# New orders of work for the steps of an attention pipeline that runs over five engines of one core

## Chip, core and metric

One NeuronCore of a Trainium2 chip runs the whole program in one launch. The metric is the device time of one execution in microseconds, median of several. The kernel before takes 427.58 us (three runs, 427.24 to 427.79). A time on the profile's clock is counted from the start of the profiled execution's span.

## What is computed

A pre-norm decoder layer over `x` of 64 sequences by 64 positions by 128 channels, in float32:

```python
x = x + attention(layernorm(x), Wv, bv, Wo, bo)        # q = k = v = layernorm(x) @ Wv.T + bv, 16 heads of 8
x = x + cross_attention(layernorm(x), ctx, ctx)        # 16 heads of 8, no projections
x = x + experts(layernorm(x), router, ...)             # one shared expert and the best one of seven, SwiGLU, 352 wide
```

Each attention is a softmax over 64 keys per head, with the scores divided by the root of the head's width.

## The kernel before

Two sequences make a **unit** of 128 rows (`U` = 32 units). The program has a first stage, both attentions and the normalised rows of the third part for all units (the profile's first 233 us, with a drain to about 262 us), and a second stage, routing and experts (to 427 us). The change is in the first stage alone.

The first stage is a software pipeline written out by hand: `phase_a` calls `body(t, u, live)` on each engine for steps t = 0 to 32, and in step t each part of the work is done for the unit t minus its lag:

```python
LAG = {"norm": 0, "xT": 0, "proj": 1, "S_s": 1, "soft_s": 2, "out": 3, "xb": 3, "q": 4, "pv_x": 5, "on_x": 6, "st_x": 7}
```

Every engine takes its instructions strictly in the order in which its own `body` issues them, and engines wait for one another by semaphores. That order, one list per engine, is all that decides how the work interleaves. `sp`, `pool`, `pe`, `act` and `dve` below are the DMA queue's engine, GpSimd, TensorE, ScalarE and VectorE.

The parts of a step, with the lines of the profile and the tiles:

- **Self attention.** TensorE turns the normalised row (`xT`, L778), projects it (L802 and L809, into `ps_v` and `ps_pT`), ScalarE copies the projections out (`pT` L1137, `v_s` L1143), GpSimd lays the keys out by heads (`k_s` L479, which the diff calls `keys_masked`). TensorE forms the self scores (L659 from `k_s,pT`, into the two banks `ps_s`), VectorE takes maxima (`mx_s`, L1361) and subtracts them (`pr_s`, L1376), ScalarE takes the exponential (L1065). TensorE turns the weights in the same two banks (L668, `turn`), ScalarE copies them out (`prT_s`, L1072, `turned`), TensorE weighs the values (L680, `weigh`), ScalarE copies the result (`oT_s`, L1078), TensorE turns it back (L690 from `oT_s`, `turn_back`), and VectorE inverts the sums and normalises (`rden_s` L1384, `on_s` L1392).
- **Through memory.** `on_s` is stored and read back as rows (`orow`), TensorE turns those (L758, `turn_output`), ScalarE copies them out (`onT`), TensorE projects them (L763, `project`), and VectorE adds the result to `x_all` (L1431).
- **Second norm.** VectorE takes moments of that sum (`st_s` L1340) and mean and variance (`mv<-st_s`, L1351, `mean_variance("s", ...)`). GpSimd subtracts the mean (`xn_s`, L497). TensorE turns the centred row (L735, `query`) and ScalarE copies it out (`qT`).
- **Cross attention** goes the same way with `x` in the names: scores from `ring,qT` (L659), maxima and subtraction of both banks at once (L1361, L1368), two turns (L668), weighing (L680 from `prT_x,ring`), turning back (L690 from `oT_x`), normalising (`on_x`), adding (L491).

TensorE uses three tile shapes: the full array (`128*128` in the rows) for turns and `project`, 64 by 64 quarters for both scores, and 128 by 32 strips for weighing and for the self projection. After step 32 the last units are finished by straight code, here called the drain. `keep_clock` issues matmuls on zeros (L647), in the first steps only.

The waits that matter below:

```python
def scores(k, u, q, keys):                 # self scores overwrite the banks in which the last unit's weights were turned
    if u >= 1:
        pe.wait_ge(sem(f"{k}_prT"), G * u)
def invert(k, u):
    dve.wait_ge(sem(f"{k}_ot"), at(u))     # the turning back
```

## Time and profile before

| | |
|---|---|
| runs | 427.58 us median of 3 |
| profiled execution, span | 427.0 us, 0.6 us under the median; the time of its launch beside the span is not given |
| first stage, steps 5 to 32 | 35.5 us to about 233 us |
| TensorE busy over the span | 404.4 us, 95% |
| VectorE, ScalarE, GpSimd busy | 71%, 70%, 67% |
| mean granted TensorE clock | full but for one stretch near 290 us |

The span of the profiled execution is what its rows add up to. The other runs are a little longer, and that difference is put on top of every sum at the end. A row of the timeline gives start, length, engine, line and tiles; its length can be longer than the distance to the next row, since an engine's instructions overlap by their ends. Distances from start to start are the surer measure.

### The profile page before, as it was taken

What the parts mean: (1) busy time and instruction counts of PE and PEld (TensorE: products, weight loads), DVE (VectorE), ACT (ScalarE), POOL (GpSimd) and SP (SyncE); (2) the same over time, 40 slices, a digit from 0 to 9 for tenths busy, and PEclk for the clock granted to TensorE, in tenths of its full rate; (3) what the DMA queues carried; (4) which work ended last, traced back from release to release, by engine and by line L of the source; (5) the groups of instructions that cost most, each with busy time, mean ns of one, the idle gap of its engine ahead of it and who ended that gap; (6) DMA issues with size and microseconds to landing.
All of it is one profiled execution on the core that took longest, in us unless ns stands there. A gap on an engine that the chain in (4) does not pass through costs nothing.

```text
span 427.0 us, 16199 instructions
## 1 busy us (share of the span) xinstructions
PE 404.4 (95%) x5545; PEld 312.9 (73%) x5546; DVE 305.1 (71%) x791; ACT 298.5 (70%) x684; POOL 284.8 (67%) x476
## 2 busy tenths in 40 slices
PE   7989999999998999999999898969999999999997
PEld 4646666666665666666665667959988999999996
DVE  7868999999998998999999787713333444444444
ACT  7659999999998999999998685302213466666651
POOL 8757788878887888888888423665664463444442
PEclk9999999999999999999999999996999999999999
DMA  6254566767676667765444300021113255430001
GB/s 104 43 85 64 87 103 108 109 110 121 120 124 117 114 123 126 143 101 84 60 63 43 35 2 2 27 81 58 69 69 90 67 133 139 131 104 27 27 32 52
DMA packets 176324, 35.22 MB, mean 82 GB/s; under 512 B 145587, under 2 KB 174646, under 8 KB 176256
## 3 DMA queue, kind: packets, MB, share of 16 engines
q1 hardware_dynamic: 71296, 21.43, 23.1%
q10 hardware_dynamic: 102144, 6.81, 15.2%
q0 software_dynamic: 2816, 6.10, 4.1%
q8 instruction: 40, 0.66, 0.7%
q14 instruction: 28, 0.23, 0.2%
HBM read 20.86 MB, written 15.67 MB: 86 GB/s over the span
## 4 chain that ended last, share of the span: by engine, by line
PE 68%; DMA 10%; issue 6%; DVE 6%; ACT 3%; SPq 2%; POOL 2%; another core or an unknown queue 2%; DVEq 0%; ACTq 0%; POOLq 0%
PE psum L867 15%; PE psum L659 12%; PE psum L668 12%; PE psum L973 8%; PE psum L680 7%; DMA orow<-attention_out 3%; DMA attention_out<-on_s 3%; PE psum L690 3%; SPq L198 2%; DMA ring<-sorted_rows 2%; PE psum L763 2%; PE psum L802 2%; PE psum L758 1%; PE psum L809 1%
## 5 line engine op out<-in xcount | busy, mean ns | idle before, releaser
L1583 DVE TENSOR_TENSOR gT<-gT,psum 128x384 f32<-128x384 f32 x66 | 36.5, 553 | 77.5 <-PE psum L867 34.4
L1263 ACT ACTIVATE gT<-psum 128x384 f32<-128x384 f32 x70 | 33.6, 488 | 58.4 <-PE psum L867 36.9
L620 POOL DMA_INDIRECT out<-yrow,token x38 | 37.1, 975 | 41.2 <-DVE yrow L1718 22.0
L973 PE MATMUL psum<-wdn_sb,gT 128*128 (+1 forms) x420 | 60.2, 280 | 4.0 <-DVE rows_all L1597 2.2
L479 POOL TENSOR_TENSOR k_s<-pT,hmask_sb 128x1024 f32<-128x1024 f32 x32 | 61.0, 1906 | 0.9 <-ACT pT L1137 0.8
L973 PEld LDWEIGHTS psum<-wdn_sb,gT 128*128 128x128 f32 x420 | 53.3, 195 | 5.7 <-issue 2.7
L867 PE MATMUL psum<-fhT,wtile 128*128 128x128 f32 x456 | 57.2, 275 | 0.3 <-ACT wtile L1292 0.3
L867 PE MATMUL psum<-hT_all,wup_sb 128*128 128x128 f32 x384 | 50.9, 283 | 5.0 <-issue 3.8
L867 PEld LDWEIGHTS psum<-fhT,wtile 128*128 128x128 f32 x456 | 53.9, 192 | 0.5 <-ACT wtile L1292 0.5
L867 PEld LDWEIGHTS psum<-hT_all,wup_sb 128*128 128x128 f32 x384 | 47.7, 198 | 6.0 <-issue 4.8
L1065 ACT ACTIVATE pr_x<-pr_x,rs 128x512 f32<-128x512 f32 x60 | 43.0, 722 | 8.2 <-DVE pr_x L1368 7.0
L1361 DVE TENSOR_REDUCE mx_s<-psum 128x16 f32<-128x1024 f32 x33 | 40.4, 1223 | 9.1 <-PE psum L659 8.3
L668 PEld LDWEIGHTS psum<-id_sb,pr_x 128*128 128x128 f32 x248 | 26.2, 141 | 25.9 <-ACT pr_x L1065 24.0
L1361 DVE TENSOR_REDUCE mx_x<-psum 128x16 f32<-128x1024 f32 x30 | 36.7, 1224 | 7.1 <-PE psum L659 7.1
L1376 DVE TENSOR_TENSOR pr_s<-psum,mx_s 128x512 f32<-128x512 f32 x64 | 40.6, 676 | 0.3 <-issue 0.3
L1065 ACT ACTIVATE pr_s<-pr_s 128x512 f32<-128x512 f32 x64 | 37.1, 624 | 3.2 <-DVE pr_s L1376 2.5
L1368 DVE TENSOR_TENSOR pr_x<-psum,mx_x 128x1024 f32<-128x1024 f32 x30 | 36.7, 1225 | 3.1 <-DVE mx_x L1361 0.4
L680 PEld LDWEIGHTS psum<-prT_x,ring 128*32 128x32 f32 x992 | 19.0, 109 | 24.8 <-issue 24.5
L1072 ACT COPY prT_s<-psum 128x512 f32<-128x512 f32 x66 | 36.2, 605 | 0.9 <-PE psum L668 0.3
L668 PE MATMUL psum<-id_sb,pr_x 128*128 128x128 f32 x248 | 36.0, 284 | 0.5 <-ACT pr_x L1065 0.5
L668 PE MATMUL psum<-id_sb,pr_s 128*128 128x128 f32 x264 | 35.1, 275 | 0.6 <-ACT pr_s L1065 0.5
L1072 ACT COPY prT_x<-psum 128x512 f32<-128x512 f32 x62 | 34.1, 587 | 1.1 <-PE psum L668 0.9
(193 smaller groups left out, 872.0 us busy)
## 6 DMA issues: line engine op xcount, KB each, us to landing
sorted_rows<-nowhere_row SPq DMA_DIRECT2D x38, 130.0 KB, 3.6
ring<-sorted_rows SPq DMA_DIRECT2D x30, 130.0 KB
wup_sb<-in_wup SPq DMA_DIRECT2D x14, 176.0 KB, 3.0
orow<-attention_out SPq DMA_DIRECT2D x31, 64.0 KB
ring<-in_ctxv ACTq DMA_DIRECT2D x60, 32.0 KB, 3.7
cross_keys<-in_ctxk ACTq DMA_DIRECT2D x14, 128.0 KB, 3.7
ring<-cross_keys SPq DMA_DIRECT2D x112, 16.0 KB
rows_all<-in_x ACTq DMA_DIRECT2D x10, 128.0 KB, 3.9
```

The lines of the kernel that those rows point to most:

```text
L479: nc.gpsimd.tensor_tensor(k_s[:], pT[:].rearrange("p (b k) -> p b k", b=NB).unsqueeze(2).broadcast_to([P, NB, HG, S]), hmask_sb[:, 0:HG].u ...
L620: pool.indirect_dma_start(out=out, out_offset=bass.IndirectOffsetOnAxis(ap=token[p][:, 0:1], axis=0), in_=yrow[p][:, :], in_offset=None, b ...
L659: last = nc.tensor.matmul(ps_s[k][g][S * b:S * (b + 1), :], q[S * g:S * (g + 1), S * b:S * (b + 1)], keys[S * g:S * (g + 1), b, :, :].rear ...
L668: last = nc.tensor.transpose(ps_s[k][g][:, i * P:(i + 1) * P], pr[k][:, g, 2 * i:2 * i + 2, :].rearrange("p h k -> p (h k)"), id_sb[:])
L680: last = nc.tensor.matmul(ps_wT[k][VW * i:VW * (i + 1), g, S * b:S * (b + 1)], values[:, VW * pair:VW * (pair + 1)], prT[k][:, g, i, S * b ...
L867: return nc.tensor.matmul(ps[p][:, c * P:(c + 1) * P], weights[:, start:start + P], tokens, start=True, stop=True)
L973: last = nc.tensor.matmul(ps_y[p], gT[place_of(n) if isinstance(n, int) and n < FIRST else p][:, c, :], wdn_sb[:, expert, c, :], start=(c ...
L1065: nc.scalar.activation(pr[k][:, g, :, :], pr[k][:, g, :, :], ACT.Exp, scale=rs[u % 2][:, 0:1] if k == "x" else float(DK) ** -0.5).then_inc ...
L1072: nc.scalar.copy(prT[k][:, g, :, :].rearrange("p i q -> p (i q)"), ps_s[k][g]).then_inc(sem(f"{k}_prT"), 1)
L1361: nc.vector.tensor_reduce(mx[k][:], both(k), AX.X, ALU.max).then_inc(sem(f"{k}_mx"), G)
L1368: nc.vector.tensor_tensor(pr[k][:], both(k), mx[k][:].unsqueeze(3).broadcast_to([P, G, HG, S]), ALU.subtract).then_inc(sem(f"{k}_sub"), G)
L1376: nc.vector.tensor_tensor(pr[k][:, g, :, :], scores_of(k, g), mx[k][:, g, :].unsqueeze(2).broadcast_to([P, HG, S]), ALU.subtract).then_inc ...
```

## The change

The first five steps (t below `STEADY` = 5) keep their orders in functions called `opening`, with two more `keep_clock` matmuls in step 3. From step 5 on all four computing engines get a new order. No arithmetic is added or taken away, except that the maxima and the subtraction of the cross scores are done one bank at a time (`maximum_of`, `soften`) where both banks were done by one instruction each. The turning of the stored rows stands at the start of a step and not at the end of the one before. The first instructions of the drain are reordered on TensorE, ScalarE and VectorE.

TensorE:

```diff
+            def body(t, u, live):
+                if t < STEADY:
+                    return opening(t, u, live)
+                if live("q"):
+                    turn_output(u["q"])
+                if live("soft_s"):
+                    turn("s", u["soft_s"], 0)
+                    turn("s", u["soft_s"], 1)
+                if live("on_x"):
+                    turn_back("x", u["on_x"])
+                if live("q"):
+                    project(u["q"])
+                if live("S_s"):
+                    self_scores(u["S_s"])
+                if live("soft_s"):
+                    self_weighed(u["soft_s"])
+                turn("x", u["pv_x"], 0)
+                if live("xT"):
+                    new_row(u["xT"])
+                turn("x", u["pv_x"], 1)
+                if live("soft_s"):
+                    turn_back("s", u["soft_s"])
+                if live("q"):
+                    query(u["q"])
+                cross_weighed(u["pv_x"], (0,))
+                if live("xT"):
+                    self_projected(u["xT"])
+                cross_weighed(u["pv_x"], (1,))
+                if live("q"):
+                    cross_scores(u["q"])
```

VectorE, the first part of a step:

```diff
+            def body(t, u, live):
+                if t < STEADY:
+                    return opening(t, u, live)
+                if live("st_x"):
+                    normalise("x", u["st_x"])
+                if live("out"):
+                    invert("s", u["out"])
+                    normalise("s", u["out"])
+                mean_variance("s", u["pv_x"] + LAG["q"], u["pv_x"])
+                if live("soft_s"):
+                    maxima("s", u["soft_s"])
+                    soften("s", u["soft_s"], 0)
+                    soften("s", u["soft_s"], 1)
...
+                maximum_of("x", u["pv_x"], 0)
+                maximum_of("x", u["pv_x"], 1)
+                soften("x", u["pv_x"], 0)
+                soften("x", u["pv_x"], 1)
```

GpSimd lays out the keys first in its step and adds the bias later; ScalarE copies the values out behind the turned self weights:

```diff
+                if live("proj") and steady:
+                    keys_masked(u["proj"])
...
+                if live("xb") and steady:
+                    bias_added(u["xb"])
```

```diff
+                if live("soft_s"):
+                    turned("s", u["soft_s"], 0)
+                    turned("s", u["soft_s"], 1)
+                if live("proj"):
+                    values_out(u["proj"])
```

In the drain on TensorE:

```diff
-            turn("s", U - 1, 0)
-            turn("s", U - 1, 1)
+            turn_output(U - 3)
             pe.wait_ge(sem("p_v"), U)
             pe.wait_ge(sem("p_pT"), U)
             turn_rows(0)
+            turn_back("x", U - 5)
             pe.wait_ge(sem("s_onT"), at(U - 3))
             project(U - 3)
+            turn("s", U - 1, 0)
+            turn("s", U - 1, 1)
```

**Where the rows stand, TensorE around the turning back.** On TensorE, in a steady step, from the self scores of one unit on, before the change (the tiles are those of the list above; line numbers are of the kernel before):

```order
L659 MATMUL psum<-k_s,pT 64x512 x4
L668 MATMUL psum<-id_sb,pr_x 128x128 x8
L690 MATMUL psum<-id_sb,oT_s 128x128 x2
L735 MATMUL psum<-id_sb,xn_s 128x128
L802 MATMUL psum<-wv_sb,xnT 32x64 x8
L809 MATMUL psum<-xnT,wv_sb 32x128 x4
L680 MATMUL psum<-prT_x,ring 32x64 x8
L659 MATMUL psum<-ring,qT 64x512 x4
L680 MATMUL psum<-prT_x,ring 32x64 x8
```

The same stretch of the changed kernel, with its own line numbers (L703 is the turning back, L748 the query, L803 and L810 the projection, L672 the scores):

```order
L672 MATMUL psum<-k_s,pT 64x512 x4
L693 MATMUL psum<-prT_s,v_s 32x64 x16
L681 MATMUL psum<-id_sb,pr_x 128x128 x4
L784 MATMUL psum<-id_sb,xn_p 128x128
L681 MATMUL psum<-id_sb,pr_x 128x128 x4
L703 MATMUL psum<-id_sb,oT_s 128x128 x2
L748 MATMUL psum<-id_sb,xn_s 128x128
L693 MATMUL psum<-prT_x,ring 32x64 x8
L803 MATMUL psum<-wv_sb,xnT 32x64 x8
L810 MATMUL psum<-xnT,wv_sb 32x128 x4
L693 MATMUL psum<-prT_x,ring 32x64 x8
L672 MATMUL psum<-ring,qT 64x512 x4
```

The turning back of the self result and the query stay neighbours; the weighing of the self values has moved behind the self scores, and the projection between the two halves of the cross weighing.

**TensorE at the start of a step.** From the turning of the stored rows to the self scores, before the change:

```order
L758 MATMUL psum<-id_sb,orow 128x128
L668 MATMUL psum<-id_sb,pr_s 128x128 x8
L763 MATMUL psum<-wo_sb,onT 128x128
L690 MATMUL psum<-id_sb,oT_x 128x128 x2
L778 MATMUL psum<-id_sb,xn_p 128x128
L680 MATMUL psum<-prT_s,v_s 32x64 x16
L659 MATMUL psum<-k_s,pT 64x512 x4
```

And in the changed kernel:

```order
L771 MATMUL psum<-id_sb,orow 128x128
L681 MATMUL psum<-id_sb,pr_s 128x128 x8
L703 MATMUL psum<-id_sb,oT_x 128x128 x2
L776 MATMUL psum<-wo_sb,onT 128x128
L672 MATMUL psum<-k_s,pT 64x512 x4
```

Two blocks, the new row's turn and the self weighing, no longer stand between the turned self weights and the self scores.

**VectorE between the sum and the maxima of the self scores.** Before the change, from the sum with the projected rows on:

```order
L1431 TENSOR_TENSOR rows_all<-psum,rows_all 128x128
L1384 RECIPROCAL rden_x<-psum 128x16
L1340 BN_STATS st_s<-rows_all 128x6
L1340 BN_STATS st_p<-rows_all 128x6
L1392 TENSOR_TENSOR on_x<-psum,rden_x 128x128
L1351 BN_AGGR mv<-st_p 128x2
L1351 BN_AGGR mv<-st_s 128x2
L1361 TENSOR_REDUCE mx_s<-psum 128x16
L1340 BN_STATS st_x<-rows_all 128x6
L1384 RECIPROCAL rden_s<-psum 128x16
```

And in the changed kernel (L1504 is the sum, L1481 the reciprocal, L1489 the normalising, L1443 mean and variance):

```order
L1504 TENSOR_TENSOR rows_all<-psum,rows_all 128x128
L1481 RECIPROCAL rden_x<-psum 128x16
L1432 BN_STATS st_s<-rows_all 128x6
L1489 TENSOR_TENSOR on_x<-psum,rden_x 128x128
L1481 RECIPROCAL rden_s<-psum 128x16
L1489 TENSOR_TENSOR on_s<-psum,rden_s 128x128
L1443 BN_AGGR mv<-st_s 128x2
L1453 TENSOR_REDUCE mx_s<-psum 128x16
```

The reciprocal and the normalising of the self result stood behind mean and variance of the sum, and now stand in front of them.

## Rows read from the trace of the kernel before

**Rows 1.** Chain that ended last, one steady step: start, us, what.
```profile
113.84 1.02 PE psum L659 x8
114.86 1.08 PE psum L668 x8
115.94 0.22 PE psum L690 x2
...
116.27 0.36 PE psum L802 x16
...
116.85 0.22 PE psum L680 x16
...
117.08 1.09 PE psum L659 x8
118.17 0.36 PE psum L680 x16
118.53 0.26 PE psum L758
118.79 0.87 PE psum L668 x8
119.67 0.32 PE psum L763 x2
...
120.31 0.59 PE psum L680 x32
120.91 0.57 PE psum L659
```

**Rows 2.** Timeline of TensorE: self scores of step 5 and of step 32.
```profile
35.47 1.09 PE L659 MATMUL psum<-k_s,pT 64*64 64x512 f32 x8
...
229.11 1.09 PE L659 MATMUL psum<-k_s,pT 64*64 64x512 f32 x8
```

**Rows 3.** Timeline: handovers from engine to engine, in brackets the idle time before.
```profile
237.82 0.38 PE L690 MATMUL psum<-id_sb,oT_x 128*128 128x128 f32 x2
238.24 0.26 DVE L1384 RECIPROCAL rden_x<-psum 128x16 f32<-128x16 f32 x1 [0.98 <-PE psum L690]
...
231.86 0.25 DVE L1384 RECIPROCAL rden_s<-psum 128x16 f32<-128x16 f32 x1
232.14 0.29 DVE L1392 TENSOR_TENSOR on_s<-psum,rden_s 128x128 f32<-128x128 f32 x1
232.35 0.17 DVE L1351 BATCH_NORM_AGGREGATE mv<-st_x 128x2 f32<-128x6 f32 x1
...
237.08 0.18 DVE L1351 BATCH_NORM_AGGREGATE mv<-st_s 128x2 f32<-128x6 f32 x1
237.37 0.61 POOL L557 TENSOR_SCALAR xn_s<-rows_all,mv 128x128 f32<-128x128 f32 x1 [1.88 <-DVE mv L1351]
...
5.14 0.46 POOL L450 TENSOR_SCALAR xn_p<-rows_all,nmean,rs 128x128 f32<-128x128 f32 x1
5.74 0.30 PE L778 MATMUL psum<-id_sb,xn_p 128*128 128x128 f32 x1 [0.33 <-POOL xn_p L450]
```

**Rows 4.** Timeline: turned self weights and their copies, step 3 and step 31.
```profile
19.96 1.26 PE L668 MATMUL psum<-id_sb,pr_s 128*128 128x128 f32 x8 [0.29 <-ACT pr_s L1065]
20.65 1.19 ACT L1072 COPY prT_s<-psum 128x512 f32<-128x512 f32 x2
...
220.56 1.09 ACT L1072 COPY prT_s<-psum 128x512 f32<-128x512 f32 x2
```

**Rows 5.** Timeline of TensorE: the row that waits for a DMA.
```profile
134.03 0.33 PE L758 MATMUL psum<-id_sb,orow 128*128 128x128 f32 x1 [1.35 <-DMA orow<-attention_out]
```

**Rows 6.** Windows: busy us of each engine, then granted clock, DMA share, GB/s.
```profile
22.00:26.00 4.00, 2.30 (x51) 0.96 (x50) 2.84 (x7) 1.91 (x6) 2.77 (x5) 1.00 0.64 123
285.50:289.00 3.50, 0.92 (x5) 0.84 (x6) 0.00 (x0) 0.12 (x1) 1.10 (x2) 0.86 0.17 57
289.00:292.00 3.00, 2.94 (x13) 2.67 (x13) 2.00 (x5) 1.14 (x3) 1.19 (x2) 0.50 0.00 0
```

More of the change, by code:

```diff
@@ L575, in _ @@
             root_s(34, U - 2)
-            add_x(U - 4)
+            cross_added(U - 4)
             root_s(35, U - 1)
@@ L763, in project, with new_row, self_weighed, self_scores @@
                 nc.tensor.matmul(ps_wo, onT[:], wo_sb[:], start=True, stop=True).then_inc(sem("s_wo"), 1)
-            def body(t, u, live):
+            def new_row(u):
+                pe.wait_ge(sem("p_xn"), at(u))
+                if u >= 1:
+                    pe.wait_ge(sem("p_v"), u)
+                    pe.wait_ge(sem("p_pT"), u)
+                nc.tensor.transpose(ps_xT, xn["p"][:], id_sb[:]).then_inc(sem("p_xT"), 1)
+            def self_weighed(u):
+                pe.wait_ge(sem("p_v"), at(u))
+                weigh("s", u, 0, v_s[u % 2][:])
+                weigh("s", u, 1, v_s[u % 2][:])
+            def self_scores(u):
+                pe.wait_ge(sem("s_khd"), at(u))
+                scores("s", u, pT, k_s)
+            def self_projected(u):
+                pe.wait_ge(sem("p_xnT"), at(u))
+                for b in range(NB):
+                    for j in range(4):
+                        h2, k = j // 2, S * b + VW * (j % 2)
+                        last = nc.tensor.matmul(
+                            ps_v[VW * j:VW * (j + 1), S * b:S * (b + 1)], xnT[:, k:k + VW],
+                            wv_sb[:].rearrange("p (a c d) -> p c a d", a=HP, c=2)[:, h2, :, :], start=True, stop=True,
+                            tile_position=(0, VW * j))
+                last.then_inc(sem("p_pv"), 1)
+                for j in range(4):
+                    rows = slice(VW * j, VW * (j + 1))
+                    last = nc.tensor.matmul(ps_pT[rows, :], wv_sb[:, rows], xnT[:], start=True, stop=True, tile_position=(0, VW * j))
+                last.then_inc(sem("p_p"), 1)
+            def opening(t, u, live):
                 if live("soft_s"):
@@ L785, in body @@
                 if live("S_s"):
-                    pe.wait_ge(sem("s_khd"), at(u["S_s"]))
-                    scores("s", u["S_s"], pT, k_s)
-                if live("pv_x"):
-                    turn("x", u["pv_x"], 0)
-                    turn("x", u["pv_x"], 1)
+                    self_scores(u["S_s"])
                 if live("soft_s"):
@@ new lines, in values_out @@
+            def values_out(u):
+                if u >= 2:
+                    act.wait_ge(sem("s_pv"), G * (u - 1))
+                act.wait_ge(sem("p_pv"), at(u))
+                for h2 in range(2):
+                    rows = slice(S * h2, S * (h2 + 1))
+                    last = nc.scalar.copy(v_s[u % 2][rows, :].rearrange("p (a b e) -> p b a e", a=HP, b=NB)[:, :, :, DK * h2:DK * (h2 + 1)],
+                                          ps_v[rows, :].rearrange("p (b a d) -> p b a d", a=HP, b=NB))
+                last.then_inc(sem("p_v"), 1)
@@ L1146, in body, with row_out, opening @@
+            def row_out(u):
+                act.wait_ge(sem("p_xT"), at(u))
+                if u >= 1:
+                    act.wait_ge(sem("p_p"), u)
+                    act.wait_ge(sem("p_pv"), u)
+                nc.scalar.copy(xnT[:], ps_xT).then_inc(sem("p_xnT"), 1)
+            def opening(t, u, live):
+                if live("proj"):
+                    keys_out(u["proj"])
+                    values_out(u["proj"])
                 if live("soft_s"):
@@ L1516, in _ @@
             normalise("x", U - 6)
-            moments_x(U - 6)
-            maxima("s", U - 1)
             invert("s", U - 2)
             normalise("s", U - 2)
+            maxima("s", U - 1)
+            moments_x(U - 6)
             mean_variance("x", 33, U - 6)
```

222 lines of the change are left out of this document (109 added, 113 removed).

## The prediction, made before the changed kernel was run

> **What bounds the kernel now.** I read the chain that ended last first. In a steady step it is TensorE and nothing else [rows 1]: from the self scores at 113.84 us to the next ones at 120.91 us the pieces follow one another, 7.07 us a step. No other engine is as full (the table above has them near 70%). So a step costs what TensorE's own instructions cost in their order, as long as every wait in front of them is met in time. I checked this with the timeline: the self scores of step 5 start at 35.47 us, those of step 32 at 229.11 us [rows 2], 193.64 us for 27 steps, where 27 times 7.07 us is 190.89. The whole first stage has lost only 2.75 us to waits. Part of it is the turned row that waits 1.35 us for its load [rows 5].
>
> That leaves two questions for any new order. How much shorter does TensorE's own list get? And does each of its instructions still find its input ready? For the second I went through the new lists with the waits in hand, row by row, for what each instruction needs and what stands in front of its producer.
>
> **What the order saves on TensorE.** The chain's pieces show what a change of tile shape costs, because the same work stands there with and without it [rows 1]. Sixteen passes of weighing take 0.22 us behind other strips and 0.36 behind the quarters (0.14 more). Eight turns take 0.87 us behind another turn and 1.08 behind quarters (0.21). The single stored row takes 0.26 behind strips where one turn of the eight is 0.11 (0.15). The projection's first part takes 0.36 behind a turn; its equal among strips is 0.22 (0.14). Going into quarters is not told apart; I keep the pieces as they are.
>
> The new list has six changes of shape instead of seven. The stored row now follows quarters (0.06 more), the cross turns follow strips (0.05 less), the first cross weighing pays the entry that the projection paid (no change), the second half of the cross weighing stands among strips (0.14 less), and the cross scores lose a small wait for `qT` (1.09 to 1.05). Together 0.2 us less, rounded: 6.87 us a step. Splitting the cross maxima and subtraction costs VectorE little and it has slack; I put it at nothing. What covers it is the 3.3 us of TensorE work between the cross scores and the cross turns. If that cover were gone it would be about a tenth of a microsecond a step.
>
> **The first new wait, the large one.** In the new order the query's row is centred by GpSimd after mean and variance of the sum, `mv<-st_s`. VectorE issues that behind the reciprocal and the normalising of the self result. And the reciprocal waits for the turning back of that same step, which TensorE issues as the last thing in front of the query. This is a matter of units: in step t TensorE turns back unit t-2 and then queries unit t-4. VectorE takes unit t-2's reciprocal and then unit t-4's mean and variance in its own step t+1. So between two neighbours in TensorE's list there is now a full round over three engines. Before, mean and variance stood in front of the reciprocal and the round didn't exist.
>
> Its length, from start to start [rows 3]: turning back to the reciprocal 0.42 us (237.82 to 238.24), reciprocal to normalising 0.28 (231.86 to 232.14), normalising to mean and variance 0.21 (232.14 to 232.35), from there to the centring 0.29 (237.08 to 237.37), the centring itself 0.61, and from GpSimd's end to TensorE 0.14 (5.60 to 5.74). Sum 1.95 us from the start of the turning back to the query. Without a wait the query starts after the 0.22 us of the turning back [rows 1]. **1.73 us of standing TensorE a step**. Bounds: each of the six handovers could be 0.05 better or worse, so 1.4 to 2.0. VectorE is there in time: laid out by hand in the same way, the work in front of the reciprocal ends some 2 us earlier (an estimate). GpSimd is too, with the new place of the keys. Queued behind the waiting query are the cross weighing, the projection of the new row and the cross scores, and with them everything in the next step. What is queued on VectorE behind the reciprocal are the maxima of the self scores, which were ready before it; they are late too, but not the last.
>
> **The second new wait.** The self scores write into the banks in which the last unit's weights were turned, so they wait for both copies of these. Before, they stood behind `project`, two turns and the self weighing. Now they stand directly behind the turned weights, one turning back and `project`: 0.87 + 0.22 + 0.32 = 1.41 us after the first turn starts [rows 1]. The copies need longer: the first starts 0.69 us after the first turn (19.96 to 20.65), the pair takes 1.09 us when nothing holds it, and a handover from ScalarE to TensorE I estimate at 0.05 [rows 4]. That is 1.83 us, so **0.42 us of waiting**. Bounds: nothing, if ScalarE's copies go faster than ever seen here, and 0.8, if ScalarE is still busy with the exponentials when the turns end. The self scores are not held by the laid-out keys, which GpSimd now does first and has ready about half a microsecond before.
>
> **The sum.** A step becomes 6.87 + 1.73 + 0.42 = 9.02 us instead of 7.07, 1.95 more. Times 27 that is 52.7. The 2.75 us of old hiccups go, since a longer step gives the store and load of the rows more room. Steps at the edges: the query of step 4 already waits behind VectorE's new step 5, between 0 and 1.7, I take 0.7; the self scores of step 5 wait 0.4; step 32 doesn't pay the large wait, since the drain begins with mean and variance, and gains 0.2. The two added clock-keeping products stand where TensorE waits for its first stored row, and cost nothing. The drain is the same work; I put its new front at 0, between -1 and +1. The second stage is the same. 427.0 + 52.7 - 2.75 + 0.7 + 0.4 - 0.2 = 477.9 us of span, and 0.6 more for the median of the runs: 478.4, I say 478. Its own range: a step adds 1.6 to 2.3 us by the bounds, which gives 469 to 488.
>
> **Where the Trainium skill would have it otherwise.** At its one wait of this kind the trace shows TensorE standing 1.35 us in front of a row whose load had not landed [rows 5], though the transposes behind it need nothing of it. The Trainium skill, "TensorE: Matmul & The Clock Gate", in the table of its head and in the section on the array of 16 parts, says that TensorE's queue can pull weight loads ahead of matmuls in flight. By that rule the weights behind the query could be in place when it is released. The trace agrees as far as it goes: nothing but loads goes ahead in the rows. By it alone the sum would be lower by no more than the 0.14 of one change of shape a step, 3.8 us.
>
> **The rivals.**
> - *TensorE works on behind the query.* If what is queued there (weighing 0.36, projection 0.22 + 0.22, second weighing 0.22, in all about 1.0 us that needs nothing of the query) were done during the wait, a step would lose 0.7 and not 1.7: 478 - 27 = 451. Against it is the idle row of [rows 5]. 3 in 100.
> - *The second wait isn't there*, the rest is: 478 - 27 x 0.42 = 467. 7 in 100.
> - *A third handover gets late* in the longer step, such as ScalarE's second store, which now is issued behind the key copy and by which the next normalising is held (it waits for both stores). A wait of 0.6 us a step gives 494. 7 in 100.
> - *The clock falls.* In one stretch TensorE had little work, 0.92 us of 3.5, and right behind it the granted clock is 0.50, the lower level of 1.2 GHz, for the next 3 us at least [rows 6]. In another it worked 2.30 us of 4 and the clock stayed at 2.4 GHz, and the new step, with one stand of 1.7 us and one of 0.4 in 9, looks like that one and not like the first. If the clock did fall once a step for 3 us, 1.5 us would be lost each time, 27 x 1.5 = 40: 519, and far more if it stayed low. 6 in 100.
> - *Not slower.* The large wait costs nothing if the query finds its row ready, that is if mean and variance are out before the turning back ends. Then the 0.2 us a step and the old hiccups are won: 427.6 - 5.4 - 2.75 = 419. It decides from where the round takes under 0.22 us; the shortest single handover of it is 0.14 and there are six. 2 in 100.
>
> **Numbers.** My own case has 75 in 100. The range reaches from 464 to 493: it takes in the missing second wait and ends below the third handover and the clock. A measurement of this kernel tells 0.2% from no change, some 0.9 us. Faster 0.02, same 0.01, slower 0.97.
>
> **What would show it.** In the changed kernel's profile the waits of TensorE should have the query (`xn_s`) released by GpSimd at the top, about 1.7 us a time and 27 times, and the self scores (`k_s,pT`) released by ScalarE's `prT_s`, about 0.4. Starts of the self scores should stand 9.0 us apart. The chain should have GpSimd's `xn_s` and VectorE's `rden_s`, `on_s` and `mv` in it once a step. TensorE's load row of [rows 5] should not wait any more. The granted clock should stay at full. I am wrong if the query follows the turning back within half a microsecond, if the step is under 8.6 or over 9.4 us, or if the clock falls in the first stage.

## The result, and the profile after

The changed kernel takes 482.43 us (median of 4 runs, 481.57 to 483.41) where the one before takes 427.69 (4 runs, 427.24 to 428.45): a ratio of 1.126, with a 95% interval of 1.123 to 1.129. It is slower, inside the forecast range and 4.4 us above the forecast.

The page of the changed kernel first. It shows what answers to the table and to [rows 1, 5]:

```profile
span 480.7 us, 16288 instructions
PE 410.8 (85%) x5549; PEld 317.0 (66%) x5550; DVE 313.3 (65%) x847; ACT 296.5 (62%) x684; POOL 283.2 (59%) x476
...
PEclk9999999999999999999989999999799899999999
...
L1481 DVE RECIPROCAL rden_s<-psum 128x16 f32<-128x16 f32 x33 | 8.5, 257 | 58.2 <-PE psum L703 58.2
L748 PE MATMUL psum<-id_sb,xn_s 128*128 128x128 f32 x32 | 10.4, 324 | 40.9 <-POOL xn_s L512 40.6
L672 PE MATMUL psum<-k_s,pT 64*64 64x512 f32 x256 | 34.9, 611 | 11.0 <-ACT prT_s L1125 11.0
```

TensorE's busy share has fallen to 85%, and two groups of matmuls now have idle time in front of them. The view of TensorE's waits, from 30 to 295 us, counts them (line waited for, us in total, times, longest):

```profile
PE psum L748 <- POOL xn_s L512: 40.6, 28, 1.8
PE psum L672 <- ACT prT_s L1125: 11.0, 28, 0.5
```

Both forecast waits stand there, 28 times each. For the query that is 1.47 us in each of the steps 5 to 31, but for one of 1.82 us, and 0.61 us in step 4, where 0.7 had been put. The wait for a stored row's load [rows 5] is gone. The timeline of one round, to be held against the handovers of [rows 3]:

```profile
156.12 0.38 PE L703 MATMUL psum<-id_sb,oT_s 128*128 128x128 f32 x2
...
156.54 0.26 DVE L1481 RECIPROCAL rden_s<-psum 128x16 f32<-128x16 f32 x1 [1.98 <-PE psum L703]
156.84 0.29 DVE L1489 TENSOR_TENSOR on_s<-psum,rden_s 128x128 f32<-128x128 f32 x1
157.04 0.17 DVE L1443 BATCH_NORM_AGGREGATE mv<-st_s 128x2 f32<-128x6 f32 x1
...
157.31 0.61 POOL L512 TENSOR_SCALAR xn_s<-rows_all,mv 128x128 f32<-128x128 f32 x1 [2.60 <-DVE mv L1443]
...
157.97 0.33 PE L748 MATMUL psum<-id_sb,xn_s 128*128 128x128 f32 x1 [1.47 <-POOL xn_s L512]
...
158.23 0.27 PEld L693 LDWEIGHTS psum<-prT_x,ring 128*32 128x32 f32 x16
```

From the start of the turning back to the query are 0.42 + 0.30 + 0.20 + 0.27 + 0.61 + 0.05 = 1.85 us. VectorE was idle for 1.98 us before the reciprocal and GpSimd for 2.60 before the centring. No engine is too slow here: each stands and waits for the one ahead of it. The last row is the first weight load of what is queued behind the query, and it too starts only after the query.

The step, from TensorE's timeline of the same kernel (the first row answers to the first of [rows 2], the last to its second):

```profile
35.84 1.09 PE L672 MATMUL psum<-k_s,pT 64*64 64x512 f32 x8 [0.54 <-ACT prT_s L1125]
...
126.33 1.09 PE L672 MATMUL psum<-k_s,pT 64*64 64x512 f32 x8 [0.39 <-ACT prT_s L1125]
135.38 1.09 PE L672 MATMUL psum<-k_s,pT 64*64 64x512 f32 x8 [0.39 <-ACT prT_s L1125]
...
281.90 1.09 PE L672 MATMUL psum<-k_s,pT 64*64 64x512 f32 x8 [0.40 <-ACT prT_s L1125]
```

A step takes 9.05 us. The 27 steps take 281.90 - 35.84 = 246.06 us against 193.64 before, 52.4 more. The way to step 5 takes 0.4 more (35.84 against 35.47), and what follows step 32 takes 198.8 against 197.9. That is the whole difference of the spans, 480.7 - 427.0 = 53.7.

One step of the first stage is different, step 27, from 234.95 to 245.70 us, 10.75 us. Its query waited 1.82 us instead of 1.47, since VectorE began mean and variance 0.54 us after the start of the normalising (238.31 to 238.85) and not 0.20. Behind it the windows show the granted clock (the number after the five busy times) at the lower level, 1.2 GHz:

```profile
240.00:241.00 1.00, 1.00 (x57) 0.93 (x56) 0.97 (x3) 0.27 (x2) 0.92 (x4) 1.00 1.05 106
241.00:242.00 1.00, 1.00 (x20) 0.26 (x8) 1.00 (x5) 0.70 (x2) 0.90 (x2) 0.59 0.53 87
...
243.00:244.00 1.00, 1.00 (x7) 1.00 (x6) 0.94 (x2) 0.34 (x2) 0.92 (x4) 0.50 0.00 0
```

Step 27 took 1.70 us more than the others. Only part of that is the clock. In a later profile of the same kernel (e12) the query of step 27 waited as long, the windows from 240 to 244 us show the clock at full, and the step took 9.40 us:

```profile
239.97 0.33 PE L748 MATMUL psum<-id_sb,xn_s 128*128 128x128 f32 x1 [1.82 <-POOL xn_s L512]
```

So the longer stand costs 0.35 us and the clock the other 1.35. The same stand was followed by a fall in one profile and by none in the other.

### The profile page after: what moved, and what is told of

It is laid out like the page before. It is cut to its first block and busy times, and to the rows that moved or that the text cites. A ratio compares the mean times of both kernels' runs of the same rounds, so it can differ in the third digit from the quotient of the medians.

```text
span 480.7 us, 16288 instructions
## 1 busy us (share of the span) xinstructions
PE 410.8 (85%) x5549; PEld 317.0 (66%) x5550; DVE 313.3 (65%) x847; ACT 296.5 (62%) x684; POOL 283.2 (59%) x476
## 3 DMA queue, kind: packets, MB, share of 16 engines
q10 hardware_dynamic: 102144, 6.81, 12.7%
## 5 line engine op out<-in xcount | busy, mean ns | idle before, releaser
L512 POOL TENSOR_SCALAR xn_s<-rows_all,mv 128x128 f32<-128x128 f32 x29 | 17.6, 607 | 77.1 <-DVE mv L1443 77.1
L919 PEld LDWEIGHTS psum<-hT_all,wup_sb 128*128 128x128 f32 x384 | 48.8, 201 | 6.6 <-issue 5.4
L1481 DVE RECIPROCAL rden_s<-psum 128x16 f32<-128x16 f32 x33 | 8.5, 257 | 58.2 <-PE psum L703 58.2
L748 PE MATMUL psum<-id_sb,xn_s 128*128 128x128 f32 x32 | 10.4, 324 | 40.9 <-POOL xn_s L512 40.6
L672 PE MATMUL psum<-k_s,pT 64*64 64x512 f32 x256 | 34.9, 611 | 11.0 <-ACT prT_s L1125 11.0
L1118 ACT ACTIVATE pr_x<-pr_x,rs 128x512 f32<-128x512 f32 x60 | 40.2, 714 | 2.9 <-DVE pr_x L1465 2.1
L681 PE MATMUL psum<-id_sb,pr_s 128*128 128x128 f32 x264 | 39.3, 289 | 1.5 <-ACT pr_s L1118 1.3
L1125 ACT COPY prT_x<-psum 128x512 f32<-128x512 f32 x62 | 36.6, 594 | 5.1 <-PE psum L681 5.0
L1458 DVE TENSOR_REDUCE mx_x<-psum 128x8 f32<-128x512 f32 x56 | 36.0, 685 | 5.0 <-PE psum L672 1.8
L681 PE MATMUL psum<-id_sb,pr_x 128*128 128x128 f32 x248 | 37.2, 280 | 0.2 <-ACT pr_x L1118 0.2
```

The lines of the kernel that those rows point to most:

```text
L672: last = nc.tensor.matmul(ps_s[k][g][S * b:S * (b + 1), :], q[S * g:S * (g + 1), S * b:S * (b + 1)], keys[S * g:S * (g + 1), b, :, :].rear ...
L681: last = nc.tensor.transpose(ps_s[k][g][:, i * P:(i + 1) * P], pr[k][:, g, 2 * i:2 * i + 2, :].rearrange("p h k -> p (h k)"), id_sb[:])
L919: return nc.tensor.matmul(ps[p][:, c * P:(c + 1) * P], weights[:, start:start + P], tokens, start=True, stop=True)
L1118: nc.scalar.activation(pr[k][:, g, :, :], pr[k][:, g, :, :], ACT.Exp, scale=rs[u % 2][:, 0:1] if k == "x" else float(DK) ** -0.5).then_inc ...
L1125: nc.scalar.copy(prT[k][:, g, :, :].rearrange("p i q -> p (i q)"), ps_s[k][g]).then_inc(sem(f"{k}_prT"), 1)
L1458: nc.vector.tensor_reduce(mx[k][:, g, :], scores_of(k, g), AX.X, ALU.max).then_inc(sem(f"{k}_mx"), 1)
```

## The experiments

They ran on three occasions. On two of them the kernel before took 415.1 and 415.7 us, on the third 428.3. The difference lies in the second stage: in the first experiment it took 184.1 us from the last steady self scores to the end, in the changed kernel above 198.8. Between 300 and 348 us TensorE is busy throughout in e1. In the same part of the changed kernel it is busy for only 1.20 us of 338 to 342 us, and the clock stands at the lower level from 342 to 346 us. So I compare by ratio, by what a kernel takes over the one before on the same occasion, and by the step (self scores to self scores). A step before takes 7.07 us, and a change of the step counts 27 times, less some 2.7 us of hiccups. Where an expectation names a time, its distance from the 427.7 us of the kernel before is what counts beside a kernel before of 415.

| kernel | us | before | ratio (95%) | step, us |
|---|---|---|---|---|
| e12 changed, again | 480.44 | 428.34 | 1.121 (1.116 to 1.126) | 9.05 |
| e5 the same rows in the kernel before | 459.45 | 415.72 | 1.102 (1.096 to 1.108) | 8.74 |
| e1 mean and variance first | 446.55 | 415.14 | 1.075 (1.072 to 1.078) | 8.31 |
| e2 weighing first | 458.40 | 415.14 | 1.104 (1.101 to 1.107) | 8.74 |
| e3 reciprocal behind the softening | 429.30 | 415.14 | 1.035 (1.031 to 1.038) | 7.64 |
| e4 e3 and e2 | 436.34 | 415.14 | 1.051 (1.048 to 1.054) | 7.92 |
| e9 e3, store late | 414.61 | 415.72 | 0.997 (0.994 to 1.000) | 7.13 |
| e10 e9 and e2 | 410.75 | 415.72 | 0.986 (0.981 to 0.991) | 6.95 |
| e8 query late | 463.77 | 428.34 | 1.084 (1.079 to 1.089) | 8.39 |
| e7 wait filled | 467.73 | 415.72 | 1.122 (1.116 to 1.129) | 9.05 |
| e6 mean and variance later | 526.49 | 428.34 | 1.229 (1.222 to 1.236) | 10.19 and more |
| e11 projection between, before | 430.82 | 428.34 | 1.006 (1.004 to 1.009) | 7.27 |

**e1: mean and variance in front of the reciprocal.** Theory A is that of the prediction: two waits, and nothing behind them. Theory B is that a second round hides behind the first. In the changed kernel, VectorE:

```diff
+                mean_variance("s", u["pv_x"] + LAG["q"], u["pv_x"])
                 if live("out"):
                     invert("s", u["out"])
                     normalise("s", u["out"])
-                mean_variance("s", u["pv_x"] + LAG["q"], u["pv_x"])
```

> The changed kernel with one row moved on VectorE: mean and variance of the sum stand in front of the self reciprocal again, all else as changed. Theory A (the two waits of the prediction are all there is): the 1.73 us in front of the query go, the 0.4 in front of the self scores stay, a step takes 7.3 us, the kernel about 433. Theory B (a second round lies hidden under the first: the maxima of the self scores stand behind the reciprocal, which waits for the turning back, so that turning back, 0.42, 0.28, 0.2, maxima 1.3, 0.7 to the exponential, 0.6 for it, must be over before the next step's turns): 4.6 us of TensorE from the turns to the turning back and 3.6 back make 8.1 to 8.2 us a step, about 456. In B TensorE waits for pr_s of ScalarE at the self turns, in A it waits for prT_s only.

The query's wait is gone, but only 0.74 us a step came back: the kernel lies 31.4 us above the one before, where theory A had 5 and theory B 28. The waits of TensorE from 60 to 230 us name another one, and the timeline of e1 shows its round:

```profile
PE psum L681 <- ACT pr_s L1118: 15.7, 20, 0.9
PE psum L672 <- ACT prT_s L1125: 8.3, 21, 0.4
```

```profile
113.14 0.38 PE L703 MATMUL psum<-id_sb,oT_s 128*128 128x128 f32 x2
113.56 0.26 DVE L1481 RECIPROCAL rden_s<-psum 128x16 f32<-128x16 f32 x1 [1.48 <-PE psum L703]
113.85 0.29 DVE L1489 TENSOR_TENSOR on_s<-psum,rden_s 128x128 f32<-128x128 f32 x1
114.06 1.21 DVE L1453 TENSOR_REDUCE mx_s<-psum 128x16 f32<-128x1024 f32 x1
115.30 1.29 DVE L1473 TENSOR_TENSOR pr_s<-psum,mx_s 128x512 f32<-128x512 f32 x2
116.03 1.23 ACT L1118 ACTIVATE pr_s<-pr_s 128x512 f32<-128x512 f32 x2 [1.16 <-DVE pr_s L1473]
...
116.71 1.25 PE L681 MATMUL psum<-id_sb,pr_s 128*128 128x128 f32 x8 [0.78 <-ACT pr_s L1118]
```

The reciprocal still waits for the turning back, and the maxima of the self scores stand behind it. They, the subtraction and the exponential make the self weights late by 0.78 us. From the turning back to the turns are 3.57 us, and from the turns to the next turning back 4.74 us of TensorE, 8.31 together, which is the step. So the reciprocal's place makes two rounds. The prediction had put the maxima down as "late too, but not the last". That holds in the changed kernel, where the first round is the longer one, and is no longer true once that is undone. Theory A falls for every repair, not for the change itself.

**e5: the same two rows in the kernel before.** Nothing else of the change: only VectorE's reciprocal and normalising, from step 5 on. The lines that take them out of their old places from then on are left out here (`...`).

```diff
+                if live("out") and t > LAG["q"]:
+                    invert("s", u["out"])
+                    normalise("s", u["out"])
                 if live("pv_x"):
                     mean_variance("s", u["pv_x"] + LAG["q"], u["pv_x"])
...
```

> The kernel before, with one thing alone: on VectorE, from step 5 on, the self reciprocal and normalising stand in front of mean and variance of the sum, as in the changed kernel. TensorE, ScalarE and GpSimd keep their old orders. Theory (the round from the turning back over VectorE and GpSimd to the query is what costs, in whatever order TensorE has the rest): 1.6 us of waiting on TensorE in front of the query in each of some 27 steps, a step of 8.7 us, the kernel 42 to 45 us above the kernel before of the same job. Rival (it costs so much only together with TensorE's new order): under 20 us above.

43.7 us above the kernel before. The timeline shows the same round in the old order of TensorE, and the same 1.47 us:

```profile
267.44 0.38 PE L690 MATMUL psum<-id_sb,oT_s 128*128 128x128 f32 x2
267.86 0.26 DVE L1384 RECIPROCAL rden_s<-psum 128x16 f32<-128x16 f32 x1 [1.74 <-PE psum L690]
...
268.63 0.61 POOL L497 TENSOR_SCALAR xn_s<-rows_all,mv 128x128 f32<-128x128 f32 x1 [2.02 <-DVE mv L1351]
...
269.30 0.33 PE L735 MATMUL psum<-id_sb,xn_s 128*128 128x128 f32 x1 [1.47 <-POOL xn_s L497]
```

By itself this one pair of VectorE's rows makes about four fifths of the loss (10.2% of 12.1 to 12.6%), 1.67 us a step of 1.98. TensorE's new order isn't needed for it.

**e2: the self weighing in front of the self scores.** It takes away the second wait alone, in the changed kernel's TensorE:

```diff
+                if live("soft_s"):
+                    self_weighed(u["soft_s"])
                 if live("S_s"):
                     self_scores(u["S_s"])
-                if live("soft_s"):
-                    self_weighed(u["soft_s"])
```

> The changed kernel with the self weighing in front of the self scores again on TensorE, all else as changed. By the prediction the wait for the copies (0.39 us a step) is covered by the first half of the weighing but for 0.06, and the wait for the query stays: 8.7 us a step, 482.4 - 27 x 0.36 = about 473. Rival: the step is set by the round over three engines as a whole and a wait taken away on TensorE only lengthens the one in front of the query: 482.

The wait for `prT_s` in front of the self scores is gone and the step is 0.31 us shorter (8.74). By starts that wait was 0.45 us. The rest of it has moved: the self weighing took 0.58 us behind the self scores and takes 0.73 here, where it starts at 105.81 us and the copies of the turned weights end only at 106.12. This order has six changes of shape too, so their number doesn't explain it.

**e3: reciprocal and normalising behind the self softening.** Both rounds of e1 are to be cut. VectorE's steady order in the changed kernel becomes:

```python
mean_variance("s", u["pv_x"] + LAG["q"], u["pv_x"])
if live("soft_s"):
    maxima("s", u["soft_s"])
    soften("s", u["soft_s"], 0)
    soften("s", u["soft_s"], 1)
if live("out"):
    invert("s", u["out"])
    normalise("s", u["out"])
```

> The changed kernel with the self reciprocal and normalising behind the maxima and subtraction of the self scores on VectorE, mean and variance in front, as it was before the change. Both theories: neither round is left, only the self scores' wait for the copies, 0.4 us. A step of 7.3 us, about 431 to 434. If it were slower than 440, some other part of the new order would be at work.

It is 14.2 us above the kernel before: the step falls to 7.64, not to 7.3. A wait of 0.20 us for the self exponential is left, and the exponential itself stands:

```profile
105.43 1.09 PE L672 MATMUL psum<-k_s,pT 64*64 64x512 f32 x8 [0.39 <-ACT prT_s L1125]
...
109.39 0.29 DVE L1489 TENSOR_TENSOR on_s<-psum,rden_s 128x128 f32<-128x128 f32 x1
...
109.71 0.62 ACTq L198 DMA_DIRECT2D attention_out<-on_s  x1
110.38 1.15 ACT L1118 ACTIVATE pr_s<-pr_s 128x512 f32<-128x512 f32 x2 [0.58 <-issue]
...
111.06 1.18 PE L681 MATMUL psum<-id_sb,pr_s 128*128 128x128 f32 x8 [0.20 <-ACT pr_s L1118]
```

ScalarE issues its second store of `on_s` (109.71) in front of the exponentials, and only behind it do they start. The store must wait for the normalising, which e3 made late. This closes a third round: self scores, maxima, subtraction, normalising, store, exponential, turns, copies, self scores. From the self scores to the turns it takes 5.63 us, from the turns to the next self scores 2.01, together the step of 7.64.

**e4: e3 and e2 together.** The diffs are those of the two.

> The changed kernel with both repairs, the VectorE order of e3 and the TensorE order of e2. The new order's six changes of tile shape instead of seven are left: 6.9 to 7.0 us a step if TensorE waits for nothing, 427.7 - 2.75 for the old hiccups - 27 x 0.15 = about 421 to 424. Rival (the shape changes save nothing, or VectorE with its split maxima becomes the bound): 427 to 430.

Missed by both: the rival's range ends some 2 us above the kernel before, and e4 lies 21.2 us above it. With the second wait gone as well the kernel is 7 us slower than e3. The timeline of e4:

```profile
108.14 1.09 PE L672 MATMUL psum<-k_s,pT 64*64 64x512 f32 x8
...
112.11 0.29 DVE L1489 TENSOR_TENSOR on_s<-psum,rden_s 128x128 f32<-128x128 f32 x1
...
113.10 1.15 ACT L1118 ACTIVATE pr_s<-pr_s 128x512 f32<-128x512 f32 x2 [1.17 <-DVE on_s L1489]
...
113.78 1.18 PE L681 MATMUL psum<-id_sb,pr_s 128*128 128x128 f32 x8 [0.79 <-ACT pr_s L1118]
```

It is the round of e3. From the self scores to the turns are 5.64 us, as there. From the turns to the next self scores are now 2.28 us instead of 2.01, since the weighing stands between them and takes longer than the wait that it replaces. That makes the step 0.28 us longer, 27 x 0.28 = 7.6 us. The wait taken out was inside the round, and TensorE stands the longer for the exponential (0.79 us instead of 0.20). The Trainium skill, "Perfetto Trace Analysis", section "Tensor Engine Instruction (MATMUL, LD_WEIGHTS)", says that ScalarE, VectorE and GpSimd are strictly first in, first out. The trace agrees: ScalarE stands 1.17 us before an exponential whose input had long been written.

**e9: e3, and ScalarE's second store behind the self exponentials.** This tests that reading alone.

```diff
-                if live("out"):
-                    second_store(u["out"])
                 if live("soft_s"):
                     exp("s", u["soft_s"], 0)
                     exp("s", u["soft_s"], 1)
+                if live("out"):
+                    second_store(u["out"])
```

> The run e3 and one more row moved: on ScalarE the issue of the second store stands behind the self exponentials, as before the change. In e3 ScalarE stood in front of the store until on_s was out, and the exponentials behind it came late (0.58 us of standing), so that TensorE waited 0.2 us and more for pr_s. Theory: that wait goes, the one for the copies stays (0.4): 7.25 us a step instead of 7.65, some 11 us under e3's distance to the kernel before, so 2 to 4 us above the kernel before of the same job. Rival (VectorE with its split maxima is the bound at 7.6): as e3, 14 us above.

Better than expected: the step is 7.13 us and the kernel 1.1 us under the one before, a difference that is hardly clear of noise. Of TensorE's steady waits only the 0.38 for `prT_s` is left. The store held 0.51 us a step in e3.

**e10: e9 and e2, all three repairs.** The diffs are those above.

> The run e4 with the second store behind the exponentials, so all three repairs: reciprocal late on VectorE, store late on ScalarE, weighing in front of the scores on TensorE. In e4 TensorE waited 0.8 us a step for pr_s, which waited for ScalarE, which waited for on_s. Theory: nothing is waited for any more but some hundredths, a step is 6.8 to 6.9 us, the kernel 6 to 9 us under the kernel before of the same job. Rival (another engine is the bound, VectorE at about 7.0): within 3 us of the kernel before.

The step is 6.95 us. The window over one step shows TensorE (first number behind the length) full, but the view of the waits of its weight loads, from 40 to 225 us, shows a wait of 0.2 us in 21 steps:

```profile
112.37:119.32 6.95, 6.94 (x137) 4.67 (x130) 6.46 (x18) 6.50 (x16) 5.81 (x11) 1.00 0.75 129
...
PEld psum L693 <- ACT prT_s L1125: 3.6, 21, 0.2
```

The kernel takes 410.75 us, 5 under the one before (1.4%, the interval 0.9 to 1.9%), where 6 to 9 were expected with 6.8 to 6.9 us a step. The loads of the second half of the self weighing wait for the second copy of the turned weights, and the weighing takes 0.80 us where the kernel before takes 0.59: the second wait of the prediction is not gone, only smaller. The rest of what is missing is a few longer steps such as one of 7.25 us, and one wait of 1.4 for the row of [rows 5], back with the short step. The gain lies in the first stage, where steps 5 to 32 take 189.55 us against 193.64. **It beats both kernels**: the new order is a gain if the reciprocal and the store don't stand where the change put them and the self weighing goes first.

**e8: the query behind both cross weighings and the projection.** Is the round long because of the engines, and can TensorE do something else meanwhile if the program says so? In the changed kernel:

```diff
-                if live("q"):
-                    query(u["q"])
                 cross_weighed(u["pv_x"], (0,))
                 if live("xT"):
                     self_projected(u["xT"])
                 cross_weighed(u["pv_x"], (1,))
                 if live("q"):
+                    query(u["q"])
+                if live("q"):
                     cross_scores(u["q"])
```

> The changed kernel with the query moved back on TensorE, behind both halves of the cross weighing and the projection, so that 1.0 us of work stands in the wait. The cross scores still need the query's copy, 0.7 us after it. The round (1.85 us from the turning back) and 0.7 put the cross scores 2.55 us behind the turning back instead of 3.14: a step of 8.45 us, 16 us under the changed kernel of this job. Rival (filling the wait brings all of the 1.0 us): 27 under it. If a step comes out at 8.3 or more the exponential's round of run e1 (8.31) is near.

The timeline of e8:

```profile
122.87 0.38 PE L703 MATMUL psum<-id_sb,oT_s 128*128 128x128 f32 x2
123.21 0.43 PE L693 MATMUL psum<-prT_x,ring 128*32 128x64 f32 x16
...
124.72 0.33 PE L748 MATMUL psum<-id_sb,xn_s 128*128 128x128 f32 x1 [0.42 <-POOL xn_s L512]
...
125.40 1.09 PE L672 MATMUL psum<-ring,qT 64*64 64x512 f32 x8 [0.35 <-ACT qT L1175]
```

From turning back to query are again 1.85 us, but now a good 1 us of them is work. 0.35 of it comes back as a wait for the query's copy. The step is 8.39 us, and the kernel takes 16.7 us less than the changed kernel of the same occasion (463.77 against 480.44). So the rival that TensorE works on behind the query is refuted twice: in the changed kernel even the weight loads behind the query came after it, at 158.23, and the same work moved ahead in the program fills the wait.

**e7: the wait filled.** Two clock-keeping products on zeros, which nothing uses, stand in front of the query. The wait in front of them, for the cross result that was normalised a round earlier, is met by then.

```diff
+                if u["pv_x"] >= 1:
+                    pe.wait_ge(sem("x_on"), u["pv_x"])
+                keep_clock(2, bank[5])
                 if live("q"):
                     query(u["q"])
```

> The changed kernel with two products on zeros in front of each query from step 5 on (0.95 us of TensorE work that nothing needs, into a bank that is free there), so that part of the wait is filled. Theory (the wait is the time of a round, and what TensorE does in it is free): still 9.05 us a step and the same 12.6% or so above the kernel before; where the clock fell once in the changed kernel's first stage, it should stay, at most 2 us gained. Rival (TensorE is the bound and the wait only fills up): 27 x 0.95, 26 us more.

The step is 9.05 us, as in e12. The products start at 111.20 us, right behind the turning back at 110.98, and run in the stand: the idle time in front of the query fell from 1.47 to 0.60 us. The time didn't move (52.0 us over the kernel before, 52.1 in e12). So the stand costs its length and nothing else. That no clock was being lost in it shows in e12 itself, whose windows have the granted clock at full through the whole first stage.

**e12: the changed kernel again,** with no edit, beside e6 and e8.

> The changed kernel as it is, beside the other runs of this job. The kernel before took 415 us where the runs e1 to e10 were made, and 427.7 beside the changed kernel. If its loss is in the steps, as the chain says, it is 52 to 54 us here too (468 beside 415) and its steps are again 9.05 us apart.

52.1 us above the kernel before. That is the distance expected, though the kernel before is at 428 us here and not at 415. The step is 9.05 and the clock didn't fall in the first stage; step 27 took 9.40 us.

**e6: mean and variance one row further back,** behind the maxima of the self scores. The round gets 1.14 us longer, as the price of one more row.

```diff
-                mean_variance("s", u["pv_x"] + LAG["q"], u["pv_x"])
                 if live("soft_s"):
                     maxima("s", u["soft_s"])
+                mean_variance("s", u["pv_x"] + LAG["q"], u["pv_x"])
+                if live("soft_s"):
```

> The changed kernel with mean and variance of the sum one row further back on VectorE, behind the maxima of the self scores (1.2 us). Theory (the round sets the step): it is lengthened by that 1.2 us and so is every step: 10.2 to 10.3 us a step, 32 to 34 us above the changed kernel of this job, more if the clock falls in the longer standing of TensorE. Rival (the loss comes from the order in general and not from this round): within 3 us of it.

46.0 us above e12, not 32 to 34. The row behind it is 27 x 1.14 = 31; the rest is the clock. A step without a fall takes 10.19 us. Four times in the 27 steps two steps in a row take 12.7 and 11.5 us, 3.8 us more for the pair, 15.3 in all. TensorE stands 2.60 us in front of the query in every step, so the length of the stand alone doesn't say when the clock falls; what else it takes is open. The windows of e6 around one stand of 2.60 us, which ends at 119.43:

```profile
117.00:118.00 1.00, 0.00 (x0) 0.00 (x0) 0.96 (x3) 0.34 (x1) 0.00 (x0) 1.00 0.17 36
118.00:119.00 1.00, 0.00 (x0) 0.00 (x0) 1.00 (x3) 0.00 (x0) 0.24 (x1) 0.84 0.26 17
119.00:120.00 1.00, 0.57 (x9) 0.35 (x13) 0.90 (x2) 0.06 (x1) 0.84 (x3) 0.50 1.20 145
```

The clock falls during the stand, and it stays at its lower level until about 125.5 us. In the next step it is low again, from about 132.3 to 135.8 us. So the fourth rival is real, but it costs this much only with a longer stand than this change makes.

**e11: the projection between the halves of the cross weighing, in the kernel before.** Only what the new list saves on TensorE:

```diff
                 if live("q"):
                     query(u["q"])
+                if live("pv_x"):
+                    cross_weighed(u["pv_x"], (0,))
                 if live("xT"):
...
                 if live("pv_x"):
-                    cross_weighed(u["pv_x"], (0,))
+                    cross_weighed(u["pv_x"], (1,))
                 if live("q"):
                     cross_scores(u["q"])
-                if live("pv_x"):
-                    cross_weighed(u["pv_x"], (1,))
```

> The kernel before with the projection between the two halves of the cross weighing on TensorE and the cross scores behind them, all other orders as before: one change of tile shape less, by the rows 0.14 us a step. Theory: 0.1 us a step is gained, 2 to 4 us in all, under the kernel before. Rival (the cross scores come 0.3 us later, VectorE and ScalarE are late for the cross turns by as much, and it is taken back): within 1 us of the kernel before, or above it.

Missed: 0.6% slower, with most steps of 7.24 to 7.31 us. The rival's time came true, but its path only in part. The cross scores now start 3.42 us after the self scores (109.82 to 113.24) and not 3.31, but behind them the timeline shows another row late, the self exponential:

```profile
113.24 1.09 PE L659 MATMUL psum<-ring,qT 64*64 64x512 f32 x8
...
113.95 0.63 ACT L1065 ACTIVATE pr_s<-pr_s 128x512 f32<-128x512 f32 x1
...
114.26 0.33 PE L758 MATMUL psum<-id_sb,orow 128*128 128x128 f32 x1
...
114.63 1.18 PE L668 MATMUL psum<-id_sb,pr_s 128*128 128x128 f32 x8
...
115.72 0.49 PE L763 MATMUL psum<-wo_sb,onT 128*128 128x128 f32 x2
```

The projection now stands behind the first half of the cross weighing, so ScalarE copies it out later, and the self exponentials behind those copies start 4.13 us after the self scores and not 3.96. The second one ends at 115.10 us, while its turns have been under way since 114.63. From the stored row to `project` TensorE takes 1.46 us, where the kernel before takes 1.03 (118.47 to 119.50). These 0.43 us are more than the order saves elsewhere. No run tests this path by itself. In the changed kernel ScalarE copies the values out behind the turned weights, and there the saving shows (e9, e10).

## Why the prediction was right, and where a term was off

*Right in its mechanism.* The round over three engines between two neighbours in TensorE's list was forecast, and it is what the trace and e5 show. VectorE was to be in time by some 2 us, and it stood idle for 1.98. That the step came out within 0.03 us is partly luck, since terms were off by up to 0.2 us against each other:

| term | said | measured |
|---|---|---|
| the round, turning back to query | 1.95 | 1.85 (156.12 to 157.97) |
| so TensorE stands | 1.73 | 1.63 |
| wait for `prT_s` | 0.42 | 0.39 idle, 0.45 by starts |
| TensorE's own list | 6.87 | 6.97 |
| step | 9.02 | 9.05 |
| edges (first steps, drain and what follows) | +0.9 | +1.3 (0.4 up to step 5, 0.9 behind step 32) |
| from the span to the median | 0.6 | 1.7 (482.43 - 480.7) |

*The handover from GpSimd to TensorE* was taken from the opening, 0.14 us [rows 3], and is 0.05 in the steady steps. That is the whole error of the round.

*TensorE's list* came out 0.1 too short, by two errors against each other. In e9's steady step 0.44 of the 7.13 us are the wait by starts, which leaves 6.69, so the order saves 0.38 us and not 0.2. But in the changed kernel the stored row and the turns of the self weights take 1.25 us instead of e9's 1.04. The turns are under way while the second self exponential still runs (it ends at 151.94 us, the turns run from 151.47 to 152.48), which the old order had hidden.

*The second wait* came out nearly right by two errors that cancel. The copies are ready 2.01 us after the first turn and not 1.83 (0.78 to the first copy, 1.08 for the pair, 0.15 to TensorE, where 0.05 had been put without a row for it), and TensorE's own work in front of the self scores takes 1.55 us and not 1.41.

*The clock* was put at no loss for the likeliest case, and it fell in one of 27 steps, for 1.35 us beside 0.35 of longer standing. That was one of the prediction's own signs of being wrong, and it came, once; in e12 it didn't. The rival of a fall in every step (519) didn't come. But e6 shows that 1.1 us more of standing brings low clock in 8 of 27 steps.

*The 4.4 us* over the forecast are then: 27 x 0.03 = 0.8 of the step, 1.7 of step 27, 0.4 at the edges, 1.1 from the span to the median, and 0.4 by which I had rounded 478.4 down. The 0.6 was the gap between one execution's span and the median of others. Within one execution the changed kernel's launch takes 2.2 us more than its span (482.94 and 480.7), the kernel before 1.8 to 1.9 (such as 415.72 and 413.9).

*What would show it.* The waits, their counts (27, and one in step 4 that the sum had too) and the 9.0 us held. The clock did not stay at full. The row of [rows 5] waits no more. The chain of waits doesn't show the round, since it reaches back from the end only through the second stage; this sign was badly chosen, and the view of waits gave it instead.

*What the prediction didn't see* is that two more rounds lie in reserve, one through the maxima (e1) and one through ScalarE's store (e3, e4). It had the store among its rivals, as a wait in the changed kernel itself. They don't touch its number but they decide what a repair is worth.

## What to carry to other kernels

If another engine's list has the producer of an engine's next instruction behind something that needs the one before it, a full round lies between the two, and it costs the sum from start to start (here 1.85 us), however idle the engines are. After taking out a wait, follow the next round through the same place before you price the repair: here the first gave back 0.7 us a step, and only the third made the order pay. Before you take a wait out, see whether it lies inside the round that sets the step: if what replaces it is longer, the step grows. An issue of a transfer that has to wait counts in its engine's list like any other row; in front of an exponential ScalarE stood for up to 1.17 us by it, and moving it was worth 0.51 us a step.

## What the runs showed of the hardware that was not expected

- The granted clock stayed at full in nearly all steps with stands of 1.47 and 0.39 us in 9.05. It fell once behind a stand of 1.82 us, and in e12 not at all behind the same stand. With stands of 2.60 us in steps of 10.19 it fell in four of the 27 steps during the stand, stayed low for some 6.8 us, and was low again for some 3.4 us in the step behind. The only case I had before it was a stretch nearly without work [rows 6].
- The same kernel before took 415 and 428 us on different occasions. No trace of it at 415 us was kept, but the kernels profiled beside it on the 415 us occasions take some 184 us behind step 32 and those on the others some 198. In the changed kernel, one of the latter, TensorE stands idle in places in the second stage and the clock dips there, and in e1 neither is so between 300 and 348 us. Why is open; no experiment bears on it.
- Taking out a wait made a kernel slower: e4 lies 7 us above e3 with one wait less on TensorE.
